# LoRA projection with selected weights on one core: low products by sample in float32, and the mixing of a quad moved into the next one

## The reference

```python
x = x + einsum('bct,bcd->bdt', x, weights[cond])        # x: 64 x 32 x 512, weights: 16 x 32 x 32
base  = einsum('bsi,oi->bso', x, W)                     # W: 512 x 512
low   = einsum('bsi,bir->bsr', x, A[label])             # A: 5 x 512 x 32, label in 0..2 here
delta = einsum('bsr,or->bso', low, B_w) * 0.5           # B_w: 512 x 32
x = x + base + delta
```

## Time and profile before

| | |
|---|---|
| median of 3 runs | 84.39 us (84.02 to 85.27) |
| profiled execution, own time | 85.05 us |
| its span in the trace | 82.9 us |
| TensorE busy | 76.3 us |
| VectorE, ScalarE, GpSimd busy | 42.9, 33.8, 25.8 us |

### The profile page before, as it was taken

The page is one execution under the profiler, slowest core; times in us unless marked ns, Lnnn a source line. Parts: engine busy times, 40 slices in busy tenths (PEclk is TensorE's granted clock), DMA queues, the critical chain, the costliest instruction groups (busy, mean ns, idle before and its releaser), DMA issues.

```text
span 82.9 us, 1563 instructions
## 1 busy us (share of the span) xinstructions
PE 76.3 (92%) x596; PEld 63.5 (77%) x596; DVE 42.9 (52%) x79; ACT 33.8 (41%) x70; POOL 25.8 (31%) x42
## 2 busy tenths in 40 slices
PE   4979999999999999999999999999999999999700
PEld 4489899999888588898885888988858887899300
DVE  3285666979932594059725950597269305202220
ACT  0625573624442286225422872254229622343320
POOL 4422786787878778750000200000003000000000
PEclk9999999999999999999999999999999999999995
DMA  0899999083280005797260049980000049705555
GB/s 9 274 270 362 172 202 159 17 209 76 70 199 16 13 11 133 207 249 223 73 180 0 0 124 219 205 214 6 0 4 0 0 95 211 201 8 111 142 127 126
DMA packets 13658, 10.18 MB, mean 123 GB/s; under 512 B 1748, under 2 KB 11348, under 8 KB 13652
## 3 DMA queue, kind: packets, MB, share of 16 engines
q1 hardware_dynamic: 12704, 9.64, 48.1%
q0 software_dynamic: 512, 0.26, 1.7%
q10 hardware_dynamic: 436, 0.20, 1.2%
HBM read 5.90 MB, written 4.19 MB: 122 GB/s over the span
## 4 chain that ended last, share of the span: by engine, by line
PE 83%; DMA 7%; SPq 4%; DVE 1%; issue 1%; DVEq 0%
PE p_u L586 16%; PE p_u L587 15%; PE p_u L588 15%; DMA x_rows<-in_x 7%; PE p_y L602 5%; PE p_low L572 5%; PE p_low L576 5%; PE p_low L571 5%; PE p_u L597 4%; SPq L209 3%; PE p_y L586 2%; PE p_y L587 2%; PE p_y L588 2%; PE p_fold L593 1%; PE p_fold L592 1%; PE p_fold L648 1%
## 5 line engine op out<-in xcount | busy, mean ns | idle before, releaser
L586 PE MATMUL p_u<-m_hi,xt_hi 128*128 128x512 f32 (+1 forms) x64 | 23.4, 365 | 0.0
L587 PE MATMUL p_u<-m_lo,xt_hi 128*128 128x512 f32 (+1 forms) x64 | 22.9, 358 | 0.0
L588 PE MATMUL p_u<-m_hi,xt_lo 128*128 128x512 f32 (+1 forms) x64 | 22.8, 356 | 0.0
L266 POOL DMA_INDIRECT w_sel<-in_L_cond_weights,w_row x16 | 16.2, 1011 | 4.6 <-issue 4.6
L428 DVE STREAM_TRANSPOSE xt<-x_sb 128x512 f32<-128x512 f32 x14 | 15.5, 1115 | 0.7 <-DMA x_sb<-in_x 0.7
L586 PEld LDWEIGHTS p_u<-m_hi,xt_hi 128*128 128x128 f32 x64 | 12.1, 189 | 4.3 <-issue 2.9
L448 DVE COPY u_sb<-p_u 128x512 f32<-128x512 f32 (+1 forms) x7 | 4.6, 654 | 18.0 <-PE p_u L597 18.0
L588 PEld LDWEIGHTS p_u<-m_hi,xt_lo 128*128 128x128 f32 x64 | 12.1, 189 | 1.9
L587 PEld LDWEIGHTS p_u<-m_lo,xt_hi 128*128 128x128 f32 x64 | 12.1, 189 | 1.3
L329 ACT ACTIVATE xt_hi<-xt 128x512 fp32r<-128x512 f32 x14 | 8.8, 630 | 4.8 <-DVE xt L428 4.7
L305 POOL TENSOR_TENSOR mix<-w_sel,fold_id 128x128 f32<-128x128 f32 x4 | 2.2, 550 | 25.4 <-PE p_y L602 25.3
(11 more groups left out here) (94 smaller groups left out, 95.7 us busy)
## 6 DMA issues: line engine op xcount, KB each, us to landing
x_sb<-in_x SPq DMA_DIRECT2D x28, 128.0 KB, 3.0
out<-y_sb SPq DMA_DIRECT2D x12, 256.0 KB, 4.0
w_sb<-in_L_cond_W SPq DMA_DIRECT2D x4, 256.0 KB, 4.3
x_rows<-in_x SPq DMA_DIRECT2D x2, 256.0 KB, 4.3
out<-y_two SPq DMA_DIRECT2D x4, 128.0 KB, 2.3
out<-y_one SPq DMA_DIRECT2D x6, 64.0 KB, 1.9
a_sb<-in_L_cond_lora_A SPq DMA_DIRECT2D x1, 256.0 KB, 6.6
w_sel<-in_L_cond_weights,w_row POOLq DMA_INDIRECT x16, 2.4
```

Of the source, the lines that this page charges most:

```text
L266: nc.gpsimd.indirect_dma_start(out=w0_sel[:, t, :], out_offset=None, in_=W0_rows, in_offset=bass.IndirectOffsetOnAxis(ap=w0_row[:, t:t + 1 ...
L586: mm(to, xt_hi[:, slot, c, rows], m_hi[:, c, cols], start=(c == 0 and half != 1), stop=False)
L587: mm(to, xt_hi[:, slot, c, rows], m_lo[:, c, cols], start=False, stop=False)
L588: mm(to, xt_lo[:, slot, c, rows], m_hi[:, c, cols], start=False, stop=False)
```

## The change

- **A by sample.** GpSimd copies the 128x128 block of A of each sample's label out of `a_sb` into `a_sel` (64 copies with an address from a register, `select_a`), 16 for a quad, in its list ahead of that quad's gathers; for quad 0 and quad 1 ahead of all of them. The differences from label 0, the mask, `lora_half`, the split of A and `fold_pair` go.
- **Low products.** `low_group` multiplies in plain float32: for each tile 4 chunks x 4 samples, with the sample's 32 rows of x as the stationary operand and 32 columns of its A as the moving one, each into 32 partitions of `p_low` (four column positions of the array). The groups are tiles (0,1), (2,3), (4..7), (8..11), (12..15). DVE repeats the result four times (`copy_low`), TensorE transposes it (`spread_low`), ACT copies it and DVE subtracts in half of the partitions (`rest_of_low`). B is transposed in the head's place by `transpose_b` after the first half of main tile 0.
- **Mixing.** Quad k-1 is mixed after tiles 4k and 4k+1, not after the low products of quad k's first pair. `u_sb` holds eight tiles instead of four.
- **The lists.** Those of ACT and DVE are written anew and unrolled, TensorE's too. SP's order of loads and stores stays; B moves to ACT's queue and A is one transfer of five labels.

```diff
-            def low_pair(slot, waits=False):
-                for c in range(C):
-                    mm(p_low[:, 0:ROWS], ad_hi[:, c], xt_hi[:, slot, c], start=(c == 0), stop=False)
-                    mm(p_low[:, 0:ROWS], ad_hi[:, c], xt_lo[:, slot, c], start=False, stop=False)
...
+            def low_group(g):
+                for t in GROUPS[g]:
+                    at = t - GROUPS[g][0]
+                    quad, half = t // 4, t // 2 % 2
+                    if t % 2 == 0:
+                        pe.wait_ge(s_a_pool, QS * quad + QS // 2 * (half + 1))
...
+                    for c in range(C):
+                        for b in range(BT):
+                            last = mm(p_low[S * b:S * (b + 1), R * at:R * (at + 1)],
+                                      xt[:, half, t % 2, c, S * b:S * (b + 1)],
+                                      a_sel[:, BT * t + b, R * c:R * (c + 1)], start=(c == 0), stop=(c == C - 1))
+            def spread_low(g):
+                pe.wait_ge(s_low_rep, g + 1)
+                for t in GROUPS[g]:
+                    last = mm(p_fold[:, P * (t % 4):P * (t % 4 + 1)], low_rep[:, t - GROUPS[g][0]], ident[:],
+                              start=(t == GROUPS[g][0]), stop=(t == GROUPS[g][-1]), is_transpose=True)
...
+            def select_a(k):
+                first = QS * k
+                _, ats = nc.values_load_multi_w_load_instructions(
...
+                for i in range(QS):
+                    nc.gpsimd.tensor_copy(a_sel[:, first + i], a_sb[:, bass.ds(ats[i], C * R)]).then_inc(s_a_pool, 1)
...
+            def begin_quad(k):
+                pe.wait_ge(s_xlo, 4 * k + 1)
+                pe.wait_ge(s_u_even, 2 * k - 1)
+                if k == 1:
+                    main_tile(p_u[0], 0, 0, chunks=(0,))
+                    spread_low(k + 1)
+                    main_tile(p_u[0], 0, 0, chunks=(1, 2, 3))
+                else:
+                    pe.wait_ge(s_u_even, 2 * k)
+                    spread_low(k + 1)
+                    main_tile(p_u[0], 0, 0)
+                pe.wait_ge(s_stack_lo, k + 2)
+                delta_tile(p_u[0], 0)
+                pe.wait_ge(s_xlo, 4 * k + 2)
+                pe.wait_ge(s_u_odd, 2 * k - 1 if k == 1 else 2 * k)
+                main_tile(p_u[1], 0, 1)
+                delta_tile(p_u[1], 1)
+                mix_quad(k - 1)
+                pe.wait_ge(s_u_even, 2 * k + 1)
+                pe.wait_ge(s_xlo, 4 * k + 3)
+                main_tile(p_u[0], 1, 0)
+                delta_tile(p_u[0], 2)
+            for k in range(1, QUADS - 1):
+                begin_quad(k)
+                main_tile(p_u[1], 1, 1, chunks=(0, 1, 2))
+                low_group(k + 2)
+                main_tile(p_u[1], 1, 1, chunks=(3,))
+                delta_tile(p_u[1], 3)
```

More of the change, by code:

```diff
@@ new lines, in _ @@
+            transpose_x(4)
+            rest_of_low(0)
+            transpose_x(5)
+            copy_u(1, p_u[1])
+            copy_low(1)
+            transpose_x(6)
+            rest_of_low(1)
+            transpose_x(7)
+            copy_low(2)
+            copy_u(3, p_y[3])
+            for k in range(1, QUADS):
+                t = 4 * k
+                more = k < QUADS - 1
+                if k == 1:
+                    split_x(4)
+                    split_x(5)
+                if more:
+                    transpose_x(t + 4)
+                rest_of_low(k + 1)
+                split_x(t + 2)
+                split_x(t + 3)
+                if more:
+                    transpose_x(t + 5)
+                copy_u(t + 1, p_u[1])
+                if more:
+                    split_x(t + 4)
+                    split_x(t + 5)
+                    transpose_x(t + 6)
+                    transpose_x(t + 7)
+                    copy_low(k + 2)
+                    copy_u(t + 3, p_u[1])
@@ L615, in mix_two @@
                     for j in range(4):
-                        last = mix_product(p_y[i], left, i, j, j // 2, halves[j % 2])
+                        last = mix_product(p_y[i], left, i, j, TILES - 4 + j // 2, halves[j % 2])
                 last.then_inc(s_y, 1)
@@ L631, in transpose_w @@
                     at = H * (c % 2) + P * (o % 2)
-                    mm(p_y[2 * half + c // 2][:, at:at + P], rows_t[:, c], ident[:],
-                       start=(k % 2 == 0 and c % 2 == 0), stop=False, is_transpose=True)
-            def lora_half(half):
-                for c in range(C):
-                    last = mm(p_y[2 * half + c // 2][:, H * (c % 2):H * (c % 2 + 1)], a_stack[:, P * c:P * (c + 1)],
-                              b_stack[:, halves[half]], start=False, stop=(c % 2 == 1))
-                    if c % 2 == 1:
+                    last = mm(p_y[2 * half + c // 2][:, at:at + P], rows_t[:, c], ident[:],
+                              start=(k % 2 == 0 and c % 2 == 0), stop=(k % 2 == 1 and c % 2 == 1), is_transpose=True)
+                    if k % 2 == 1 and c % 2 == 1:
                         last.then_inc(s_m, 1)
@@ L650, in transpose_rows, with transpose_b @@
                 last.then_inc(s_rows_t, 1)
+            def transpose_b(bank):
+                pe.wait_ge(s_bw_rep, 1)
+                for o in range(OC):
+                    last = mm(bank[:, P * o:P * (o + 1)], bw_rep[:, o], ident[:],
+                              start=(o == 0), stop=(o == OC - 1), is_transpose=True)
+                last.then_inc(s_bT, 1)
             pe.wait_ge(s_warm, 1)
```

510 lines of the change are left out of this document (209 added, 301 removed).

## The result

The changed kernel takes **92.21 us** (median of 4 runs, 91.84 to 93.01) against 84.83 for the kernel before (4 runs): ratio 1.092, 95% interval 1.078 to 1.106. Forecast were 84.8 us and a range up to 89.5, so the time lies outside it. The profiled run took 91.84 us, its span is 89.8 (82.9 before).

The account below looks back on a forecast made before the run. TensorE, without gaps, was taken as the bound. From the profiled 85.05 us: -13.4 + 8.8 - 0.9 (head) - 0.3 (end) + 5.9 (waits) + 0.3 (GpSimd) gave 85.45, less 0.66 to the median, 84.8; range 82.2 to 89.5.

Parts of the forecast that it names:

- The list of TensorE: Low products and folds leave, 13.4 us; new low products 6.1, spread_low 2.2 and transpose_b 0.5 come in, together 8.8.
- that rival: Low products: column positions don't run side by side with all 128 rows in use; +6.4, 91.2 us, chance 0.08.
- The head: Before the first main product: without lora_half and with x and W issued earlier, it starts at about 9.85, -0.9 us.
- Wait 1: Deltas of tiles 0 and 1, about 20.1: TensorE waits for rest_of_low of group 0 on DVE, about 0.8 us.
- wait 2: Main tile 4, about 27.1: its split by ACT stands behind the copy of tile 2's u, 1.9 us.
- GpSimd: Copies of A at 0.35 us, register loads at 1.3, ready at 26.2; low_group(2) waits 0.3 for the last copy.
- A rival with a chance of 0.27: GpSimd becomes the bound at low groups 0 and 2: slower copies give 87.0 us, register loads of 3.2 give 88.6.
- Wait 3: Delta of tile 8, about 47.4: load 6, behind quad 0's stores, holds up DVE; TensorE waits 3.2 us (1.8 to 5).
- Clock at 1.00 throughout: Sign to check over the whole kernel: TensorE's granted clock never falls, so the sum had no term for it.
- a rival of 2.0 us with a chance of 0.09: The clock falls in the wait at tile 8's delta: some 4 us at half rate give 2 back, 86.8 us.
- Behind the last mixing nothing changes: End of the kernel: the time from the last mixing on stays as before, no term in the sum.
- last wait: Last mixing's wait of 0.52 us for DVE's copy: delta and copy hide behind the first small mixing, -0.3.

Follow-up runs that it names:

- f: Changed kernel with SyncE issuing load 6 ahead of the stores of quad 0: 83.85 us, 0.983 of the kernel before on the same chip.
- e: The changed kernel itself, unedited, run again beside the kernel before on another chip: 92.12 us, ratio 1.082.
- h: Changed kernel with load 6 first, splits of tiles 4 and 5 earlier, and low products issued 32 at a time: 84.67 us, 0.994 of the kernel before.
- a: Changed kernel with load 6 ahead of the stores of quad 0, on a slower chip: 97.25 us, 1.010 of the kernel before there.
- t: Changed kernel with load 6 first, splits of tiles 4 and 5 earlier, and all low products issued twice: 107.58 us, 1.146 of the kernel before.

## Why the prediction was wrong

**The list of TensorE: right.** 13.4 us out and 8.8 in gave -4.6; measured is -3.8 between first main product and last mixing. The low products: a piece of 64 shows 0.76 us, (0.76 - 0.2)/63 = 8.9 ns from half to half, 0.28 a tile against 0.27; a whole group with both changes of tiling 1.39 against 1.43. Four column positions run side by side with all 128 rows in use, and that rival is out:

```profile
15.48 0.76 PE L564 MATMUL p_low<-a_sel,xt 128*32 128x32 f32 x64
...
43.78 1.36 PE L564 MATMUL p_low<-a_sel,xt 128*32 128x32 f32 x128
```

It is also nearly three times under the floor of about 25 ns from start to start in the Trainium skill ("TensorE: Matmul & The Clock Gate", on the back-to-back gap); measured across positions, the floor doesn't hold.

**The head: right in kind**, -1.6 against -0.9: its last transposes start 1.0 us earlier (8.71 instead of the 9.70 of the earlier trace rows), and 0.35 was counted for that. Why it is 1.0 is open.

**Wait 1 and wait 2: right**, 0.61 at 20.09 against 0.8, 1.70 at 29.29 against 1.9.

**GpSimd: not the bound.** A copy starts every 0.24 us, not every 0.35. Three of the four loads of 16 registers took 1.28, 1.06 and 1.06 us, where 1.3 was taken, and the fourth, at 44.9, took 3.20 (timeline of POOL with the idle time before 16 copies, and the line of the loads with shortest, median and longest in ns):

```profile
15.43 2.35 POOL L297 TENSOR_SCALAR w_row<-cond_all,row_of 32x16 int32<-32x16 f32 x4
19.39 3.84 POOL L276 COPY a_sel<-a_sb 128x128 f32 x16 [1.61 <-issue]
```

```profile
L271 POOLq TENSOR_LOAD <-a_at x4: 1055/1171/3195, 10.1 to 44.9; - x4
```

The copies were through at 23.2, not 26.2. The Trainium skill's 200 ns a register ("Runtime: NRT & Kernel Launch", Instruction fetch mechanics) would give 3.2 us a load. Here only the fourth load took that, in this run and in f (3.15; 2.41 in e), and every other load in all runs took 1.05 to 1.29; these loads are from SBUF. The fourth is for the low products at 65.7 and nothing waited for it. A rival with a chance of 0.27 rested on the price of the load.

**Wait 3: the right place, mis-sized**, and this is the first step that failed: 5.1 us (5.4 in e) against 3.2, a little outside its own range of 1.8 to 5. The term that was too small is the load: from the end of the stores' issue to the landing it had 4 x 0.45 + 3.0 = 4.8 us, and the trace has 6.9 (45.8 to 52.7). Right behind the stores the first two issues took 1.23 and 1.16 us, more than the longest of the earlier trace rows (0.99), and the last transfer landed 3.85 behind the start of its issue, which was within those rows (6.8 at most). A load that is issued right behind 1 MB of stores is not the median load. In the kernel before load 6 stood behind the same stores of the earlier trace rows, but was issued at 39.66, 3.1 us after them, and its four issues took 0.46 at most.

**"Clock at 1.00 throughout": the second step that failed**, and the largest: 3.2 us in the profiled run and 2.7 in e, for which the sum had nothing. It had stood as a rival of 2.0 us with a chance of 0.09, and behind wait 3 alone. The earlier trace rows showed the fall behind the last product, with the engine empty. Nor is it the wait's length by itself: after a wait of 1.69 the clock stayed up in e and fell in the run shown above and in f, after the same one.

**"Behind the last mixing nothing changes": the third**, 1.7 us, of which 0.75 is only the last mixing coming sooner.

Put into the sum, 85.45 + 1.9 (wait 3) + 3.2 (clock) + 1.7 (end) + 0.8 (list) + 0.5 (the gap in the low products) - 0.7 (head) - 0.4 (waits 1 and 2) - 0.3 (GpSimd) - 0.2 (last wait, 0.5 for 0.3) = 91.95, against 91.84 measured. The chances were wrong too: the three that failed were taken one by one, though the clock hangs on the waits, and both add up.

## What to carry to other kernels

When an edit delays a store, look at what stands behind it in the same queue: here one line of SyncE's list, load 6 ahead of `store(0)`, turned 8% slower into 2% faster on the chip of e to h, and with the splits moved as well into 4% faster. On the chips where the low products had gaps, the gain of that line alone isn't shown. A wait of TensorE costs more than its length, because the products behind it may run at half clock: count it with each long wait that an edit adds. Keep small products of another tiling together in long pieces.

## What the runs showed that was not expected

TensorE probably ran out of instructions. On four of the five chips (that of e to h is the exception), where the kernel before too took 11 us longer, low products came 4 or 5 at a time, one burst in 0.75 us. Timeline of PE in a:

```profile
24.26 0.99 PE L564 MATMUL p_low<-a_sel,xt 128*32 128x32 f32 x62
25.74 0.27 PE L564 MATMUL p_low<-a_sel,xt 128*32 128x32 f32 x4 [0.49 <-issue]
26.50 0.27 PE L564 MATMUL p_low<-a_sel,xt 128*32 128x32 f32 x4 [0.49 <-issue]
```

The engine waits for nothing that is in the program. The instruction queue in the profile page's list of DMA queues points at the loading of code, though no run shows that it is the cause: 4 packets of 16 KB before, 8 in the changed kernel (596 products and 1000), 12 in t (1512).

```profile
q8 instruction: 8, 0.13, 0.6%
```

```profile
q8 instruction: 12, 0.20, 0.8%
```

512 products more, each with a weight load, are four packets more, which makes 256 instructions to a packet (an estimate from these counts). By it a low group of 128 products is one packet, used up in 1.4 us, while products of 512 columns use one in 29 us. On the chip of e to h the same kernel had no such gap. On these four chips engines that waited for TensorE also went on up to 4 us after its record of the product had ended (the "remote" above); I have no cause for either.
